# An RWKV layer and a mixture of experts in one kernel: the first chunks in another order, and the last layer norm's scales taken for three blocks

## The reference

```
x = x + layernorm(attn(layernorm(x)))
x = x + layernorm(ffn(layernorm(x)))
```

## Time and profile before

| | |
|---|---|
| median of 3 runs | 1613.29 us (1612.08 to 1614.66) |
| the profiled execution | 1613.5 us; span from its first to its last instruction 1611.7 us |
| busy share of the span | PE 94%, DVE 85%, ACT 83%, POOL 67% |
| chain that ended last | PE 61%, POOL 16%, issue 11%, DVE 5% |
| mean granted clock of PE | 0.974 of full speed |

### The profile page before, as it was taken

The page is one execution under the profiler, slowest core; times in us unless marked ns, Lnnn a source line. Parts: engine busy times, 40 slices in busy tenths (PEclk is TensorE's granted clock), DMA queues, the critical chain, the costliest instruction groups (busy, mean ns, idle before and its releaser), DMA issues.

```text
span 1611.7 us, 35130 instructions
## 1 busy us (share of the span) xinstructions
PE 1518.8 (94%) x9960; PEld 1363.9 (85%) x9960; DVE 1377.9 (85%) x3140; ACT 1335.3 (83%) x2768; POOL 1082.7 (67%) x1168
## 2 busy tenths in 40 slices
PE   4899999999999999999999999689999998999992
PEld 3778888888888888888888888578999998999992
DVE  4799999999999999999989988856877777999993
ACT  3688898889888998999899888756777777999993
POOL 1146767767776777677667766756666664888886
PEclk9899999999999999999999999879999999999996
DMA  3112533343322222222322222228778763777771
GB/s 112 53 47 78 169 107 125 116 153 121 109 88 87 85 78 92 87 82 80 104 76 88 81 81 69 68 79 284 237 241 249 238 217 123 233 232 228 234 236 55
DMA packets 124619, 214.41 MB, mean 133 GB/s; under 512 B 19975, under 2 KB 67338, under 8 KB 124432
## 3 DMA queue, kind: packets, MB, share of 16 engines
q1 hardware_dynamic: 92368, 126.13, 26.5%
q0 software_dynamic: 32064, 86.04, 14.5%
HBM read 116.37 MB, written 99.39 MB: 134 GB/s over the span
## 4 chain that ended last, share of the span: by engine, by line
PE 61%; POOL 16%; issue 11%; DVE 5%; ACT 2%; DMA 1%; POOLq 0%; DVEq 0%; ACTq 0%; SPq 0%
PE PS L1453 51%; POOL d_ys L589 8%; POOL out L607 6%; PE PS L1445 3%; PE PS L1517 2%; PE PS L1515 2%; PE PS L1671 2%; POOL rsw L601 1%; PE PS L1687 1%; POOL d_xd L548 1%; DMA out<-vv,wqh 0%; POOL varw L599 0%; DVE st L1060 0%; PE PS L1652 0%; PE PS L1537 0%
## 5 line engine op out<-in xcount | busy, mean ns | idle before, releaser
L548 POOL DMA_INDIRECT d_xd<-h2n,ixs x248 | 312.0, 1258 | 193.8 <-DVE h2n L1178 127.6
L1453 PE MATMUL PS<-hTh,wqh 128*128 128x512 f32 x768 | 307.1, 400 | 16.0 <-ACT kk L644 10.8
L1453 PE MATMUL PS<-hTl,wqh 128*128 128x512 f32 x768 | 306.7, 399 | 0.0
L1453 PE MATMUL PS<-hTh,wql 128*128 128x512 f32 x768 | 306.2, 399 | 0.0
L1453 PEld LDWEIGHTS PS<-hTh,wqh 128*128 128x128 f32 x768 | 146.7, 191 | 50.9 <-ACT kk L644 11.7
L1453 PEld LDWEIGHTS PS<-hTh,wql 128*128 128x128 f32 x768 | 146.6, 191 | 34.5
L1453 PEld LDWEIGHTS PS<-hTl,wqh 128*128 128x128 f32 x768 | 146.8, 191 | 33.4
L555 POOL DMA_INDIRECT d_xs<-ysh,ixs x124 | 131.2, 1058 | 45.7 <-issue 45.4
L1687 PE MATMUL PS<-weh,h2h 128*128 x380 | 106.3, 280 | 0.0
L1687 PE MATMUL PS<-weh,h2l 128*128 x380 | 106.3, 280 | 0.0
L1687 PE MATMUL PS<-wel,h2h 128*128 x380 | 106.1, 279 | 0.0
(11 more groups left out here) (328 smaller groups left out, 5715.2 us busy)
## 6 DMA issues: line engine op xcount, KB each, us to landing
xin<-in_L_attn_x SPq DMA_DIRECT2D x32, 512.0 KB, 4.2
x<-in_L_attn_x SPq DMA_DIRECT2D x32, 512.0 KB
wqh<-d_xd SPq DMA_DIRECT2D x60, 272.0 KB, 3.6
wql<-d_xd SPq DMA_DIRECT2D x60, 272.0 KB, 3.4
d_xd<-zt SPq DMA_DIRECT2D x18, 272.0 KB
wel<-in_L_ffn_w SPq DMA_DIRECT2D x16, 256.0 KB, 5.1
d_xd<-h2n,ixs POOLq DMA_INDIRECT x248, 2.5
kk<-d_xs SPq DMA_DIRECT2D x12, 256.0 KB
```

Source lines behind the costliest of these rows:

```text
L548: g.indirect_dma_start(d_xd[s], bass.IndirectOffsetOnAxis(ap=ixs[:, m % 2, k:k + 1], axis=0), h2n_of(m)[:, j, :], None).then_inc(s_sct[s], 16)
L1453: ins = mm_(out_ap, l, r, start=(k == 0), stop=(k == len(todo) - 1))
```

## The change

At the start, SP loads chunk 1's rows as soon as chunk 0 is normed, ahead of the wait for the weights; `u` and `decay` get a semaphore of their own (`s_wu`); on ACT `x_normed(0)` stands before the first weight cast and `x_normed(1)` before the wait for all weights; on DVE `stats_in(1)` stands in the weight work; and the steps `i` = 0 to 2 of ACT and DVE are written out in another order (ACT: `beta(0)` before `v_out(0)`, `x_normed(2)` last; DVE: `running_max(0)`, `step_up(0)`, then `stats_in(2)`, `turned_low(1)`). PE's list is unchanged. At the end, scales are taken for groups of blocks, `SIZES`: 22 groups of three, one of two, three of one; `final` comes in step `t = v + 71 + 7`; `xk` gets six buffers.

```
-    NPAIR = (NB1 + 1) // 2
+    SIZES = [3] * ((NB1 - 5) // 3) + [2, 1, 1, 1]
+    STARTS = [sum(SIZES[:q]) for q in range(len(SIZES) + 1)]
+    NXK = 6
...
-        sqw = sb("sqw", [P, NPR, 4])
-        varw = sb("varw", [P, NPR, 4])
-        rsw = sb("rsw", [P, NPR, 4])
-        mh4 = sb("mh4", [P, 4])
+        sqw = sb("sqw", [P, NPR, 6])
+        varw = sb("varw", [P, NPR, 6])
+        rsw = sb("rsw", [P, NPR, 6])
+        mh6 = sb("mh6", [P, 6])
...
-        xk = [... for t in (ysh, xin) for i in range(2)]
+        xk = [... for t in (ysh, xin, hf) for i in range(2)]
...
+        def group_of(v):
+            q = max(g for g in range(len(SIZES)) if STARTS[g] <= v)
+            return q, v - STARTS[q]
...
@@ SP
                 for i, v in enumerate((u_in, decay)):
-                    sp.dma_start(vec[:, 3 + i, :], ...).then_inc(s_vec, 16)
+                    sp.dma_start(vec[:, 3 + i, :], ...).then_inc(s_wu, 16)
...
+            sp.wait_ge(s_nx, n(0, NT, NT))
+            sp.dma_start(xin[:, :, :], x_v[1]).then_inc(s_x, 16)
             sp.wait_ge(s_wl, NP)
             sp.dma_start(x1[:, :, :], x_v[0]).then_inc(s_xr, 16)
             for i in range(NCH + 4):
...
-                if 0 < i < NCH:
+                if 1 < i < NCH:
                     sp.wait_ge(s_nx, n(i - 1, NT, NT))
                     sp.dma_start(xin[:, :, :], x_v[i]).then_inc(s_x, 16)
...
@@ POOL
             def last_scale(q):
-                many = min(2, NB1 - 2 * q)
-                at = slice(0, 2 * many)
-                pool.wait_ge(s_sqw, 2 * (2 * q + many))
+                at = slice(0, 2 * SIZES[q])
+                pool.wait_ge(s_sqw, 2 * STARTS[q + 1])
                 if q >= NPR:
-                    pool.wait_ge(s_fin, 4 * (q - NPR + 1))
+                    pool.wait_ge(s_fin, 2 * STARTS[q - NPR + 1])
...
-            for q in range(NPAIR + 1):
-                if q < NPAIR:
-                    last_scale(q)
-                for v in (2 * q - 2, 2 * q - 1):
-                    if 0 <= v < NB1:
-                        tokens_out(v)
+            last_scale(0)
+            for v in range(NB1):
+                if v + 1 < NB1 and group_of(v + 1)[1] == 0:
+                    last_scale(group_of(v + 1)[0])
+                tokens_out(v)
...
@@ ACT
-            act.wait_ge(s_vec, 16 * 5)
-            A.activation(posw[:, :], vec[:, 4, :], ACT.Exp).then_inc(s_aprep, 1)
             act.wait_ge(s_const, NCONST)
-            copy(lowb[:, :], lowf[:, :]).then_inc(s_aprep, 1)
+            x_normed(0)
             high_mix(0, al)
-            x_normed(0)
             high_mix(1, be)
             high_mix(2, ee)
             turned_high(0)
+            act.wait_ge(s_wu, 16 * 2)
+            A.activation(posw[:, :], vec[:, 4, :], ACT.Exp).then_inc(s_aprep, 1)
+            copy(lowb[:, :], lowf[:, :]).then_inc(s_aprep, 1)
...
+            x_normed(1)

             act.wait_ge(s_prep, 7)
             act.wait_ge(s_wl, NP)

-            for i in range(NCH + 2):
+            k_out(0)
+            A.preload_act_table(ACT.Silu)
+            r_tanh(0)
+            A.preload_act_table_set("natural_log_exp_and_others")
+            beta(0)
+            v_out(0)
+            turned_high(1)
+            alpha(0)
+            own_exp(0)
+            x_normed(2)
+
+            for i in range(3, NCH + 2):
...
             def back_second(v):
-                if v >= 4:
-                    act.wait_ge(s_fin, 2 * (v - 3))
+                if v >= NXK:
+                    act.wait_ge(s_fin, 2 * (v - NXK + 1))
...
@@ DVE
             stats_in(0)
-            dve.wait_ge(s_vec, 16 * 5)
+            dve.wait_ge(s_vec, 16 * 3)
             V.tensor_scalar(omm[:, :, :], ...).then_inc(s_prep, 1)
-            dve.wait_ge(s_aprep, 1)
-            V.tensor_scalar(negw[:, :], posw[:, :], -1.0, None, ALU.mult).then_inc(s_prep, 1)
-            dve.wait_ge(s_prep, 2)
+            dve.wait_ge(s_prep, 1)
             mix(0)
...
             low_mix(2)
+            stats_in(1)
+            dve.wait_ge(s_aprep, 1)
+            V.tensor_scalar(negw[:, :], posw[:, :], -1.0, None, ALU.mult).then_inc(s_prep, 1)
...
-            for i in range(NCH + 2):
+            dve.wait_ge(s_prep, 2)
+            running_max(0)
+            step_up(0)
+            stats_in(2)
+            turned_low(1)
+
+            for i in range(3, NCH + 2):
                 if on(i - 5):
                     route(i - 5)
-                if on(i - 3):
+                if i > 3 and on(i - 3):
                     step_up(i - 3)
...
-            for t in range(NB + 6):
+            for t in range(NB + 7):
...
-                if t - 6 >= NB1:
-                    final(t - 6 - NB1)
+                if t - 7 >= NB1:
+                    final(t - 7 - NB1)
```

More of the change, by code:

```diff
@@ L209, in rwkv_moe @@
         s_vec = sem("s_vec")
+        s_wu = sem("s_wu")
         s_rwf = sem("s_rwf")
@@ L339, in rwkv_moe @@
         assert len(xb) == NX and len(yb) == NYB
-        xk = [flat(t)[:, i * 2 * D:(i + 1) * 2 * D].rearrange("p (j d) -> p j d", j=2) for t in (ysh, xin) for i in range(2)]
+        xk = [flat(t)[:, i * 2 * D:(i + 1) * 2 * D].rearrange("p (j d) -> p j d", j=2) for t in (ysh, xin, hf) for i in range(2)]
+        assert len(xk) == NXK
         xTh = [hTh[:, 0, 0:TC], rkh[:, 0, :]]
@@ L475, in _ @@
             g.memset(zero[:, :], 0.0).then_inc(s_const, 1)
-            g.memset(mh4[:, :], -0.5).then_inc(s_const, 1)
+            g.memset(mh6[:, :], -0.5).then_inc(s_const, 1)
             g.memset(ext[:, :, :, :], 0.0).then_inc(s_const, 1)
@@ L592, in last_scale @@
             def last_scale(q):
-                many = min(2, NB1 - 2 * q)
-                at = slice(0, 2 * many)
-                pool.wait_ge(s_sqw, 2 * (2 * q + many))
+                at = slice(0, 2 * SIZES[q])
+                pool.wait_ge(s_sqw, 2 * STARTS[q + 1])
                 if q >= NPR:
-                    pool.wait_ge(s_fin, 4 * (q - NPR + 1))
+                    pool.wait_ge(s_fin, 2 * STARTS[q - NPR + 1])
                 g.tensor_scalar(varw[:, q % NPR, at], sqw[:, q % NPR, at], 1.0 / D, EPS, ALU.mult, ALU.add).then_inc(s_vaw, 1)
                 pool.wait_ge(s_vaw, q + 1)
-                g.tensor_tensor(rsw[:, q % NPR, at], varw[:, q % NPR, at], mh4[:, at], ALU.pow).then_inc(s_rsw, 1)
+                g.tensor_tensor(rsw[:, q % NPR, at], varw[:, q % NPR, at], mh6[:, at], ALU.pow).then_inc(s_rsw, 1)
             def tokens_out(v):
@@ L900, in last_squares @@
             def last_squares(v):
-                w, q, k = NB1 + v, v // 2, v % 2
+                w = NB1 + v
+                q, k = group_of(v)
                 if q >= NPR:
@@ L913, in back_second @@
                 act.wait_ge(s_xb[w % NX], 16 * (w // NX + 1))
-                if v >= 4:
-                    act.wait_ge(s_fin, 2 * (v - 3))
-                A.activation(xk[v % 4][:, 1, :], xb[w % NX][:, 1, 0:D], ACT.Identity, bias=xb[w % NX][:, 1, C_EXT + 1:C_EXT + 2],
+                if v >= NXK:
+                    act.wait_ge(s_fin, 2 * (v - NXK + 1))
+                A.activation(xk[v % NXK][:, 1, :], xb[w % NX][:, 1, 0:D], ACT.Identity, bias=xb[w % NX][:, 1, C_EXT + 1:C_EXT + 2],
                              scale=xb[w % NX][:, 1, C_EXT:C_EXT + 1]).then_inc(s_backa, 1)
@@ L1389, in back @@
                 w = NB1 + v
-                if v >= 4:
-                    dve.wait_ge(s_fin, 2 * (v - 3))
-                V.tensor_scalar(xk[v % 4][:, 0, :], xb[w % NX][:, 0, 0:D], xb[w % NX][:, 0, C_EXT:C_EXT + 1], xb[w % NX][:, 0, C_EXT + 1:C_EXT + 2],
+                if v >= NXK:
+                    dve.wait_ge(s_fin, 2 * (v - NXK + 1))
+                V.tensor_scalar(xk[v % NXK][:, 0, :], xb[w % NX][:, 0, 0:D], xb[w % NX][:, 0, C_EXT:C_EXT + 1], xb[w % NX][:, 0, C_EXT + 1:C_EXT + 2],
                                 ALU.mult, ALU.add).then_inc(s_back, 1)
             def final(v):
-                w, q, k = NB1 + v, v // 2, v % 2
+                w = NB1 + v
+                q, k = group_of(v)
                 dve.wait_ge(s_rsw, q + 1)
```

5 lines of the change are left out of this document (3 added, 2 removed).

## The result

The changed kernel takes 1633.66 us (median of 4 runs, 1632.16 to 1638.48) where the kernel before took 1613.79 on the same chip: a ratio of 1.0131, 95% interval 1.0111 to 1.0151. It is slower by 20 us; 1605.5 was forecast, with a range that ended at 1610.5.

A forecast was written before the change was run, and what follows sets the result against it. TensorE was taken to bound the middle, DVE the second pass, so only the two ends could pay: 1613.5 - 10.5 (head) + 2.2 (end) + 0.5 (ring of buffers), less 0.2 for the median, gave 1605.5 us; range 1601 to 1610.5.

The forecast's parts named there:

- The head: Start of the kernel: reordered loads and steps bring later stages earlier, -10.5 us in sum, bounds -6 to -12.5.
- the pause ahead of chunk 1's product: Start: TensorE waits some 4.7 us there, ended by DVE's low part; the product starts at 42.0 instead of 50.34.
- the waits of 1.77 and 1.19 us: Start, ahead of chunk 0's out product and chunk 2's first product: they go, -2.9 us.
- The restart: TensorE at chunk 1's first product, after the new pause: slow clock loses 2.4 us (bounds 1.7 and 3.05), +0.7.
- a whole cold start: Same restart, by the skill page: the longer pause costs 3.05 us, making the sum 0.6 us more.
- The end proper: Last blocks, set by POOL's queue: +2.2 us in sum, bounds +0.9 to +4.3.
- the single scales: Last nine blocks: one pair scale and three single ones replace two pair scales and one single, +0.9 us.
- block 62's scatter: Start of the end: the scale of blocks 63 to 65 ahead of it pushes it to 1576.4, +1.4 us.
- The step that failed: Second pass over the blocks: DVE's instructions are the same, so its pace stays, 0 us.
- 9.9 us of work in 10.3: Second pass: POOL's load for three blocks, 3 x 2.68 + 1.84 us, fits within 10.3 us.
- the ring of the rival: Second pass, 12 block buffers: late scatters delay loads and DVE waits once per turn; 12 us lost, 1617; chance 0.07.

The follow-up runs named there:

- e14: New start and six `xk` buffers with the old end (pairs, sixth turn, old scale place), but single scales for the last three blocks: 1604.37 us, ratio 0.9950.
- e1: The changes of the start alone, with the end of the kernel before: 1603.08 us, ratio 0.9965 to the kernel before.
- e8: e1 with one more small POOL operation (128x4) in every pair, for which nothing waits: 1604.73 us, ratio 0.9959.
- e15: Changed kernel with pairs for threes, rings of 13 blocks and the scale two blocks sooner in POOL's queue; last product still in the seventh turn: 1604.70 us.
- e13: e12 with rings of 13 blocks for both loads instead of 12: 1615.50 us, ratio 1.0012.
- e6: e1 with the scale of each pair one block later in POOL's queue, no instruction added or removed: 1611.35 us, ratio 0.9994.
- e12: Changed kernel with pairs for threes and the scale one block sooner in POOL's queue; last product still in the seventh turn: 1615.21 us, ratio 1.0016.
- e3: Changed kernel with groups of two blocks and a single one last, instead of threes; `final` still one iteration later: 1615.35 us, ratio 1.0018.
- e2: The changes of the end alone, with the start of the kernel before: 1642.44 us, ratio 1.0195.
- e10: Changed kernel with rings of 13 blocks for both loads and nothing else: 1640.32 us, ratio 1.0171.
- e4: Changed kernel, still threes, with `final` back in the iteration it had before the change (t - 6): 1640.01 us, ratio 1.0184.
- e5: Changed kernel with the scale of each next group issued one block sooner in POOL's queue: 1628.77 us, ratio 1.0077.
- e16: e15 with the changed kernel's threes instead of pairs: 1626.43 us, ratio 1.0081.
- e9: e5 with rings of 13 blocks for both loads instead of 12: 1627.96 us, ratio 1.0091.
- e11: Changed kernel with DVE's copy of the weights' low part cut to 16 of 512 columns in the second pass: 1609.67 us, ratio 0.9985.

## Why the prediction was wrong

**The head was right.** First product 17.83 (17.6 forecast), V of chunk 0 with no wait, the pause ahead of chunk 1's product 5.82 us (4.7), ended by DVE's low part, the product at 43.00 (42.0), the waits of 1.77 and 1.19 us gone, the later stages earlier by 9.8 (10.5). In the sixteen traces with the new start the second pass begins anywhere from 1311.9 to 1319.0, so the 0.7 us between the two says little. The missing microsecond at chunk 1's product is in SP's queue: `xin` of chunk 2 went out at 34.70, not 33.7.

```profile
34.70 0.47 SPq L423 DMA_DIRECT2D xin<-in_L_attn_x  x1
```

The restart ran at a granted 0.56 in the mean of 6.00 us after the pause of 5.82 (0.50, the lower of the clock's two levels, from 43 to 48, and 1.00 from 49), which loses 2.6 us; 2.4 was taken, between the two rows.

```profile
43.00:49.00 6.00, 6.00 (x16) 4.70 (x17) 5.93 (x9) 2.08 (x4) 0.50 (x2) 0.56 0.30 85
```

By the Trainium skill's page TensorE: Matmul & The Clock Gate, Part 1, a paused array starts cold, at 1.2 of 2.4 GHz. The trace agrees, with 0.50 from the first product on; the loss lies between the 2.4 that the sum took and the 3.05 that it named for a whole cold start, nearer to the first.

**The end proper was half right.** The nine last blocks take 29.26 us (1594.53 to 1623.79) where they took 28.2: +1.06, where +0.9 was forecast for the single scales. In e14, which changes nothing else there, the time from the last low part on is 0.9 longer than in e1. But block 62's scatter starts 4.6 us after the last low part and not 1.4, because POOL arrives there late, and DVE waits for its scales:

```profile
1604.49 0.88 DVE L1431 SCALAR_TENSOR_TENSOR x<-x,rsw,ysh 128x256 f32<-128x256 f32 x2 [3.74 <-POOL rsw L611]
```

**The step that failed** is one sentence: "DVE's instructions are the same, so its pace stays: 0", with the "9.9 us of work in 10.3" for POOL beside it. It measured +24.8 us. Two readings behind it were wrong. From 100.00 us of 100 for DVE I concluded that POOL does not set the pace, and POOL's 81.73 in the same row looks like slack; but its idle fifth is nearly all the 0.2 to 0.3 us ahead of every scatter, and its pair was 6.88 us beside DVE's 6.88. The row was at hand: 6.87 us without a break, which I put down to the end alone. And I took a scatter's duration from one alignment, 2.68 us for a block with its gaps, and carried it to another. It is no constant: mostly 1.02 to 1.21 in the kernel before, 1.19 to 1.63 in the changed kernel's bad stretches, and 0.97 to 0.99 at its shortest, beside an idle DVE at the end but also beside a full one (the first rows below). With the long ones the three blocks cost 12.09 us.

DVE's own pace did not stay either, even where it waits for nothing. In the changed kernel the third turn of the pass took 3.65 us instead of 3.44, as the instruction that brings back the residual took 0.62 and not 0.40:

```profile
1357.27 0.40 DVE L1420 TENSOR_SCALAR ysh<-wql 128x256 f32<-128x256 f32 x1
...
1360.71 0.62 DVE L1420 TENSOR_SCALAR ysh<-wql 128x256 f32<-128x256 f32 x1
```

Between blocks 12 and 64 of all traces only this one (up to 0.66) and the copy of the weights' low part (0.41, up to 0.68) are stretched by more than 0.1 us.

Here are the second and the fifth block of the pass; at the fifth the changed kernel leaves its first alignment:

```profile
1355.82 0.99 POOL L617 DMA_INDIRECT out<-kk,wqh  x1 [1.06 <-DVE kk L1431]
1357.12 0.98 POOL L617 DMA_INDIRECT out<-kk,wqh  x1 [0.31 <-issue]
...
1366.35 1.60 POOL L617 DMA_INDIRECT out<-dl,wqh  x1 [1.14 <-DVE dl L1431]
1368.25 1.60 POOL L617 DMA_INDIRECT out<-dl,wqh  x1 [0.30 <-issue]
```

Both scatters begin just after the last product that they wait for; the one takes 0.99 us, the other 1.60. From then on POOL lags, by 2.7 to 4.5 us for most of the pass; three times late loads hold DVE up and POOL comes back to 0.8 us, and each time it falls behind again.

What the runs show in place of the failed step: POOL has no slack in this pass, and whether it keeps up is decided by how its scatters fall against DVE's instructions. Pairs have an alignment that holds (lags 2.7 and 3.4, scatters 1.09): before, e1, e8 with shifted values, e14, e15. It is reached when POOL's queue has the wait for the squares ahead of the scatters of blocks already finished (e15 against e13, which differ in that alone). With the scale one block later (e6), or with the last product one turn later (e12, e13), or with both (the changed loop, e3), POOL starts with a lag of 0.8. Pairs ran at full pace from there too, until a disturbance, at block 21 in e3 and 31 in e6, e12 and e13. Threes lost it without one that shows, at block 4 in the changed kernel, e2 and e10, and at block 1 in e4. For threes no order tried was good: with the scale late POOL's scatters stretch and DVE waits for the scale (the changed kernel, e4, e10); with the scale early POOL waits for a third block's squares and the loads come late (e5, e16; e9 has long scatters besides). That is the ring of the rival, which had the right sign and, at 1617, not the size; e4 and e10 show that it is not the cause in the changed kernel itself.

The rule that I did not weigh is in the Trainium skill, GPSIMD Engine Reference, Key points: GpSimd shares its SBUF interfaces with VectorE, and contends with VectorE's instructions in a two-port mode or with two SBUF inputs. The traces agree in kind: scatters of 0.97 us with DVE idle at the end, up to 1.63 beside it, 1.08 in the mean once the copy is cut, and DVE's copy stretched in turn. That section gives no size, and it does not tell why a scatter beside the same instructions took 0.99 in one turn and 1.60 in another.

**Open.** Why two scatters with the same start against DVE take 0.99 and 1.60. Over all traces but e11's, in turns under 3.48 us up to block 61, the start decides much but not all: of the scatters that began 1.30 to 2.20 us after the end of DVE's last product 363 of 364 took under 1.15 us, of those at 0.86 to 1.00 all 73 took 1.52 to 1.60, and of those at 0.74 to 0.80 278 took under 1.15 and 93 about 1.6. Open too are which form of DVE's instructions stretches them (e11 takes away the copy and DVE's full load together); whether threes with a ring of more than 13 would hold; and how often the good alignment is lost, since passes, scatters and waits are those of one execution for each kernel: two of e1's ten runs took 1613.5 and 1615.3 us, and neither was profiled.

## What to carry to other kernels

Before work is called hidden on an engine, follow one whole cycle of it on the timeline: POOL was 82% busy and had not 0.1 us to spare, as the rest was nearly all the gap of 0.2 to 0.3 us ahead of each scatter. A duration that was read beside another busy engine holds only for that alignment, so a change that shifts two engines against each other needs bounds from the shortest and the longest row of that instruction, not the mean. In the second pass before they were 0.97 and 1.37; six scatters of 1.37 would have made 11.7 us of three blocks (6 x 1.37 + 3.48), more than DVE's 10.32, and the changed kernel went on to 1.63. When the pace hangs on an alignment, the order of waits in the in-order queue is part of the design: here the place of one scale, with no work added, was worth some 10 us, and the version to keep is the new start with the old end (e1, 0.9965; e14 and e15, 0.995, are within its interval).

## What was not expected of the hardware

An indirect scatter of one and the same shape took from 0.97 to 1.63 us, and in seven of the sixteen kernels now and then 1.64 to 1.99, in the main by where it fell in DVE's turn; the 128x6 power took 1.35 and in places 1.68. Adding 0.27 us of work to a POOL that was full cost 0.11 a pair, as the scatters shortened and DVE's two turns grew by the 0.11. And in nine of the sixteen kernels the second scatter of block 30 or 31 started 0.5 to 1.8 us after the first had ended (0.3 elsewhere), always near that block, the gap ended by a last product or by nothing that the trace shows; in e6, e12 and e13 the lags of 0.8 and 1.4 us, and with them the full pace, ended there. Its cause was not found.
